# Mixed order of two kinds of score matmuls, and the fp8 rounding moved two places later on GpSimd

## The reference

```python
# x: (16, 512, 256)
x = x + attn(layernorm(x), qkv_w, qkv_b, proj_w, proj_b)   # softmax(q k^T / 4) v, 16 heads
h = clip(layernorm(x) / input_scale, -448, 448)
h = h.astype(float8_e4m3fn).astype(float32) * input_scale
x = x + h @ (weight_fp8 * weight_scale).T + bias
```

## Time and profile before

| | |
|---|---|
| time, median of 3 runs | 1026.58 us |
| lowest, highest | 1014.63, 1032.14 us |
| the profiled execution: its time, its span | 1026.58 us, 1024.1 us |
| PE busy | 952.6 us, 93% of the span |
| DVE busy | 850.2 us, 83% |
| ACT busy | 663.2 us, 65% |
| POOL busy | 523.9 us, 51% |
| mean granted clock of PE | 0.958 |

### The profile page before, as it was taken

One profiled execution on the slowest core, in us unless ns is written; L12 is line 12 of the kernel. 1 busy time (PEld: TensorE's weight loads), 2 busy tenths in 40 slices (PEclk: granted clock), 3 DMA queues, 4 the chain that ended last, 5 costly groups with the idle time before them and its releaser, 6 DMA issues.

```text
span 1024.1 us, 16767 instructions
## 1 busy us (share of the span) xinstructions
PE 952.6 (93%) x5828; PEld 481.1 (47%) x5828; DVE 850.2 (83%) x1250; ACT 663.2 (65%) x1209; POOL 523.9 (51%) x533
## 2 busy tenths in 40 slices
PE   3788999999999999999999999999999999999884
PEld 2543454554545454545444454454545454443333
DVE  3577889898989899898988899898988989798515
ACT  3136777667677767767667767776677767666630
POOL 3321446647382846637383845637383855425242
PEclk9679999999999999999999999999999999999955
DMA  5971545536254555526255554626354553601010
GB/s 149 131 110 32 84 64 105 84 60 116 51 104 71 83 84 93 97 55 112 52 103 75 88 85 84 105 54 107 50 100 69 84 85 58 107 6 43 2 41 20
DMA packets 46452, 79.42 MB, mean 78 GB/s; under 512 B 10144, under 2 KB 13344, under 8 KB 46368
## 3 DMA queue, kind: packets, MB, share of 16 engines
q1 hardware_dynamic: 46368, 78.36, 44.7%
HBM read 18.42 MB, written 8.39 MB: 26 GB/s over the span
## 4 chain that ended last, share of the span: by engine, by line
PE 60%; POOL 25%; DVE 7%; issue 5%; ACT 2%; DMA 1%; SPq 1%; POOLq 0%; DVEq 0%; ACTq 0%
PE ps_o L505 17%; PE ps_s L487 14%; PE ps_t L471 11%; POOL parts L972 5%; PE ps_m L421 5%; PE ps_m L397 5%; PE ps_m L385 3%; POOL hq L1014 3%; POOL hn L1010 3%; POOL h L1004 3%; POOL hn L994 3%; PE ps_m L453 2%; POOL parts L970 2%; POOL oT_p L956 2%; DVE mx L715 2%
## 5 line engine op out<-in xcount | busy, mean ns | idle before, releaser
L593 ACT ACTIVATE pt<-ps_t 128x512 f32<-128x512 f32 x1024 | 557.3, 597 | 253.7 <-PE ps_t L471 246.8
L715 DVE TENSOR_REDUCE mx<-ps_s 128x2 f32<-128x1024 f32 x512 | 609.1, 1207 | 37.5 <-PE ps_s L487 32.4
L505 PE MATMUL ps_o<-pt,vt 128*32 128x512 f32 x2048 | 279.0, 618 | 0.0
L487 PE MATMUL ps_s<-ks,qs 48*128 48x512 f32 x1024 | 259.3, 501 | 16.2 <-DVE nmax L764 9.4
L471 PE MATMUL ps_t<-qs,ks 50*128 50x512 f32 x1024 | 249.2, 422 | 8.8 <-ACT pt L593 8.7
L487 PEld LDWEIGHTS ps_s<-ks,qs 48*128 48x128 f32 x1024 | 98.1, 186 | 280.4 <-issue 149.7
L471 PEld LDWEIGHTS ps_t<-qs,ks 50*128 50x128 f32 x1024 | 146.7, 189 | 49.8 <-ACT pt L593 36.6
L981 POOL TENSOR_TENSOR on<-ot,rden 128x256 f32<-128x256 f32 x63 | 39.1, 621 | 248.7 <-DVE rden L776 248.7
L385 PE MATMUL ps_m<-xnT_p,wqkv_p 128*128 128x512 f32 x360 | 104.8, 420 | 1.0 <-POOL xnT_p L950 1.0
L972 POOL TENSOR_TENSOR parts<-parts 128x512 f32<-128x512 f32 x60 | 80.9, 1349 | 4.9
L505 PEld LDWEIGHTS ps_o<-pt,vt 128*32 128x32 f32 x2048 | 40.8, 109 | 76.7 <-issue 76.0
(11 more groups left out here) (94 smaller groups left out, 809.3 us busy)
## 6 DMA issues: line engine op xcount, KB each, us to landing
qs<-parts SPq DMA_DIRECT2D x192, 128.0 KB, 4.5
ks<-parts SPq DMA_DIRECT2D x192, 128.0 KB, 5.3
xin<-in_x SPq DMA_DIRECT2D x16, 512.0 KB, 3.6
xres<-in_x SPq DMA_DIRECT2D x16, 512.0 KB, 4.3
out<-h SPq DMA_DIRECT2D x32, 256.0 KB, 2.0
qs<-nmax SPq DMA_DIRECT2D x256, 4.0 KB
pt<-in_qkv_wT SPq DMA_DIRECT2D x1, 768.0 KB, 5.6
pt<-in_proj_wT SPq DMA_DIRECT2D x1, 256.0 KB, 5.6
```

Source lines behind the costliest of these rows:

```text
L487: done = nc.tensor.matmul(ps_s[:, s % 2, g, :], qs[par][rows, slot, queries], ks[par][rows, slot, :], start=True, stop=True)
L505: last = nc.tensor.matmul(ps_o[32 * i:32 * i + VW, :], vt[par][:, 2 * kp + a, head, :], pt[n % 2][:, i, a, :], start=(kp == 0 and a == 0), ...
L593: nc.scalar.activation(pt[n % 2][:, w % 2 + 2 * a, w // 2, :], ps_t[:, a, :], ACT.Exp, scale=SCALE).then_inc(exp_done, 1)
L715: dve.tensor_reduce(mx[:, r, :, s % QUARTER], ps_s[:, s % 2, :, :], AX_X, ALU.max).then_inc(max_done, 1)
```

## The change

On PE the four score matmuls of a step alternate: T for group 0, S for group 1, T for group 1, S for group 0. The waits stay with their instructions. On POOL `round_fp8(u-3)` goes from its place before `split(u, 2)` to behind `out_divide(u-2, 2)`. No instruction is added or removed.

```diff
             def slot(u, par, present):
                 for s in range(STEPS):
                     bt, st = (u - 2, s + HALF_STEPS) if s < HALF_STEPS else (u - 1, s - HALF_STEPS)
+                    if 0 <= bt < B:
+                        scores_t(bt, bt % 2, st, 0)
                     if present(1):
                         scores(u - 1, 1 - par, s, 1, True, False)
+                    if 0 <= bt < B:
+                        scores_t(bt, bt % 2, st, 1)
+                    if present(1):
                         scores(u - 1, 1 - par, s, 0, False, True)
-                    if 0 <= bt < B:
-                        scores_t(bt, bt % 2, st, 0)
-                        scores_t(bt, bt % 2, st, 1)
...
                 if present(0) and u > 0:
                     split(u, 1)
-                if present(3):
-                    round_fp8(u - 3)
-                if present(0) and u > 0:
                     split(u, 2)
                 if present(2):
                     out_divide(u - 2, 2)
+                if present(3):
+                    round_fp8(u - 3)
                 if present(0) and u > 0:
                     split(u, 3)
```

## The result

The changed kernel takes 1069.2 us (median of 4, 1067.2 to 1070.7) where the kernel before takes 1024.05 us beside it (median of 4, 1014.6 to 1032.1). The ratio is 1.047, 95% interval 1.039 to 1.055: slower, close to the 1073 us of the forecast. The profiled execution has a span of 1067.7 us, before 1024.1 us.

A forecast was written before the change was run, and what follows sets the result against it. PE sets the pace. A steady slot changes by 2.73 - 0.75 - 1.0 = +0.98 us; with the other slots +15.4 on 1026.6 gives 1042, plus 31 for clock falls behind 14 stalls: 1073 us, range 1038 to 1088.

The forecast's parts named there:

- wait at the second linear piece: PE's wait there for DVE's L812 goes, as PE arrives later: -0.75 us a steady slot.
- saving of the mixed order in a steady slot: On PE, earlier T results shorten waits for ACT's exponentials: -1.0 us, between 0 and -1.5.
- price of the stall in a steady slot, clock held: PE waits for hq at the transposes, +2.73 us, less 0.75 at the second linear piece.
- price of the clock in a slot: Half clock on PE behind each of 14 stalls, 2.2 us each, 31 us in sum.
- the follow-on of the move: On POOL, split 2 costs nothing; rounding behind the divide, which awaits rden, brings PE hq at 526.55, not 523.82: +2.73 us.
- The sentence on the Trainium skill: The skill lays clock falls to gaps longer than this stall; by it the clock holds, 1042 us; the forecast doubted it.
- The rival of 1042 us: First rival: the stall comes but PE's clock holds; 1036 to 1047 us, at 1042; chance 17%.
- slots 16 and 17 together: Kernel's end without the clock: slot 16 at +3.4 us, slot 17 stalls by some 1.4.
- the waits of the T loads for ACT: Over the whole kernel, PE's T weight loads wait less for ACT: from 36.6 us to under 20.
- The S results come later for DVE: S results come 0.2 us later; DVE has 6 us to spare in a slot, so no cost.
- The rival by which the mixed pairs are faster in the array: Second rival: pairs on PE at 0.24 us, not 0.34; 998 us at full clock, 1029 with falls; chance 10%.
- the second rival's sum: Faster pairs save 2.9 us a slot against +0.98: 17 less in 13 slots, some 45 with slots 1, 2 and 16.

The follow-up runs named there:

- e1: Mixed order on PE alone, POOL as in the kernel before; 1011.5 us, ratio 0.992 to the kernel before.
- e2: Move of round_fp8 on POOL alone, PE in the order of the kernel before; 1068.2 us, ratio 1.048 to the kernel before.
- e3: Changed kernel plus 10 useless matmuls (20 in slot 16) on PE ahead of the wait for hq; 1029.6 us, ratio 1.012 to the kernel before.
- e4: Changed kernel, but the rounding stands between split 2 and out_divide 2; 1007.8 us, ratio 0.988 to the kernel before.
- e8: Changed kernel plus 10 useless matmuls ahead of the wait for hq in slots 3 to 8 only; 1055.5 us, measured once.
- e7: Changed kernel plus 4 useless matmuls on PE ahead of the wait for hq; 1055.2 us, ratio 1.033 to the kernel before.

## Why the prediction was right, point by point

| step | forecast | measured |
|---|---|---|
| `values` of step 11 to the transposes of `hq` | 7.8 us | 8.0 (533.61 to 541.61) |
| idle time of POOL ahead of the divide | 1.5 to 1.9 | 1.43 |
| idle time of PE at the transposes, both edits | 2.9 | 3.04 |
| the move alone, PE in the old order | 2.73 | 2.73 |
| wait at the second linear piece | gone | gone |
| saving of the mixed order in a steady slot | 1.0 | alone 1.15 (e1: 0.60 + 0.55), beside the stall 0.58 (59.43 - 58.85) |
| price of the stall in a steady slot, clock held | 1.98 (2.73 - 0.75) | 1.50 (e2) |
| a slot if the clock holds | 58.9 | 58.85 (e3) |
| price of the clock in a slot | 2.2 | 2.6 (61.44 - 58.85) |
| stalls behind which the clock falls | 14 of 15 | 14 |
| time | 1073 us | 1069 us |

The step that carried the sum was the follow-on of the move: `split` 2 costs nothing, since POOL idles afterwards anyway; the whole price comes from putting the rounding behind the reciprocal, which hangs on PE's own step 11. In e4 `split` 2 alone stands ahead of the rounding; a stall of 1.02 us is left there, but no loss. And e2 shows that this edit alone makes the loss.

That the slot with a held clock came out at 58.9 us is in part luck. Two of its terms were off by some 0.45 us each, in opposite directions: the stall costs 1.50 and not 1.98, and beside it the order saves 0.58 and not 1.0. Two things tie them together. The forecast let the new order shorten the wait of the T pair in step 15; the stall removes it already in the old order. From the first pair of that step to its `values` it is 1.12 us before, 0.89 in e1 and 0.66 in both e2 and e3. And what the order saves between `values` of step 11 and the transposes is no gain beside the stall: the idle time is 3.04 us where it is 2.73 in the old order.

The two terms that were judged and not read, whether the clock falls and what that costs, are shown by e3 and e8: with the stall almost without idle time the loss shrinks from 45 us to 9, and from the transposes of slot 3 to those of slot 16, where the end of the kernel plays no part, from 45.1 to 13.7 us. The sentence on the Trainium skill (TensorE: Matmul & The Clock Gate, "Why this matters for your kernels") is decided by the measurement, though not by the changed kernel: its idle gaps, 3.04 us where 2.9 was forecast, are about as long as those that the page warns of. Gaps of 2.73 us in e2 brought the clock down in 8 of 12 slots and gaps of 1.8 us in e7 in 9 of 12, and these are shorter than the page warns of. The rival of 1042 us, by which the clock holds, was wrong in its condition.

That rival's own sum was also off, and this is a mis-sized term: e3, which meets its condition, took 1029.6 us and not 1042. The middle fits (12 slots of 58.86 us against 57.93, +11 us). The end does not: I put slots 16 and 17 together at +4.8 us; from the transposes of slot 15 to the end of the span e3 took 5.2 us less than before. Of that stretch the part from the transposes of slot 16 on is 88.6 us where before took 96.4. In the run of before the clock was at 0.50 for most of slot 17, in e3 it held until past the transposes of that slot. The stretch of before:

```profile
969.00:995.00 26.00, 22.98 (x85) 9.01 (x89) 3.38 (x6) 10.97 (x20) 13.54 (x10) 0.50 0.11 32
```

The changed kernel was low there as well, from 1009 on, so its own total fitted. What puts the clock low or high in that slot, where PE has no S pairs any more, was not tried; executions that differ in it may be why the kernel before spreads over 17 us.

One sign was wrong. I wrote that the waits of the T loads for ACT would fall from 36.6 us to under 20; they rose to 195 us, and to 204.5 in e1, whose slots are shorter than before. The reading was at fault: the first weight load of a step waits while the matmuls of the step before still run, and the wait is booked to whichever load comes first. Before, that was S: its loads waited 280 us in all and those of T 50. In e1 it is T: 301 us, and 16 for S. PE itself waits for ACT 10.7 us in e1 (8.7 before).

The S results come later for DVE, as said, and it cost nothing: DVE's waits for them rose from 32.4 to 50.4 us by the order alone (e1), while PE's own wait for DVE's maxima at L487 stayed small (4.3 us before, 2.5 in e1). Most of the 112 us of the changed kernel is the stall, for in e2, in the old order, they are 80.5.

The rival by which the mixed pairs are faster in the array is out: the second pair starts 0.34 us behind the first as before. PE's timeline of the changed kernel, one step:

```profile
551.90 0.50 PE L471 MATMUL ps_t<-qs,ks 50*128 50x512 f32 x1
551.90 0.49 PE L487 MATMUL ps_s<-ks,qs 48*128 48x512 f32 x1
552.24 0.39 PE L471 MATMUL ps_t<-qs,ks 50*128 50x512 f32 x1
552.24 0.40 PE L487 MATMUL ps_s<-ks,qs 48*128 48x512 f32 x1
```

In the second rival's sum one number doesn't follow from its terms: 2.9 us a slot in 13 slots is 38 and not 17. The total of some 45 with slots 1, 2 and 16, and so the 998 and 1029 us, goes with the 38.

## What to carry to other kernels

When an instruction is moved later in a list, find what it now stands behind and what that hangs on: here a swap of neighbours put the bound engine's own input behind a value that hangs on that engine's work three steps earlier. On PE, price a stall twice, once for the idle time and once for the clock that it can bring down; here the second part was 2.6 of the 3.5 us that a slot lost. And a gain on the bound engine can vanish in the next wait behind it; moving POOL's add of the bias ahead turned 0.8% into 3%.

## What the runs showed of the hardware that was not expected

- The same idle time has several prices. With 2.73 us at the transposes in every slot (e2) a slot took 59.4, 60.8 or about 62 us; with 1.8 us (e7) 58.8, 60.1 or 61.4. 1.02 us (e4) did no harm in any slot up to 15.
- Such a slot can lock. With both edits the transposes come 61.40 to 61.48 us apart in eleven slots on end, and each of their half-clock stretches begins 0.4 to 0.5 us ahead of the transposes. In e7 the last five steady slots take 61.43 to 61.44 us, after seven shorter ones that wandered between 58.8 and 60.1. Once a stall and a fall meet in this way, the slot seems to repeat it; what sets that length was not tried.
- A matmul of no use can be worth its time: about 2.6 us of them in a stall saved 2.6 us of a slot behind it.
